# Softmax of the gate logits in PSUM: maxima, subtraction by an identity matmul and exponential per 510-column unit; residual kept in SBUF; clamp on GpSimd

## The reference, cut to what matters

```
h = layernorm(x) * (1 + ca) + sa
n = rmsnorm(h, norm_w)                                  # M = 16, H = 8
v = n @ W_v.T                                           # 128 values
gates = softmax((n @ W_a.T).reshape(B, T, H, M, M + 1)) # 128 rows of 17 logits per token
new = A_t @ state + a0 * v                              # the scan: 512 steps over T, per batch and head
x = x + ga * (h + ys @ W_out.T)
h = layernorm(x) * (1 + cb) + sb
logits = h @ router_w.T + router_b; the best 4 of 8 experts, softmax of their logits
gate, up = split(h @ gate_up.T + bias); gate = min(gate, 7); up = clip(up, -7, 7)
act = (up + 1) * gate * sigmoid(1.702 * gate); y = sum of weight_e * (act @ down_e.T + bias_e)
x = x + gb * y
```

## Time and profile before

| | us |
|---|---|
| median of 3 runs | 946.82 (946.27 to 947.31) |
| the profiled execution, whole | 945.81 |
| its span | 944.1 |
| mean granted TensorE clock | 0.818 of full |
| busy DVE, TensorE, ScalarE, GpSimd | 836.2, 641.1, 529.3, 517.0 |

### The profile page before, as it was taken

The page is one execution under the profiler, slowest core; times in us unless marked ns, Lnnn a source line. Parts: engine busy times, 40 slices in busy tenths (PEclk is TensorE's granted clock), DMA queues, the critical chain, the costliest instruction groups (busy, mean ns, idle before and its releaser), DMA issues.

```text
span 944.1 us, 11922 instructions
## 1 busy us (share of the span) xinstructions
PE 641.1 (68%) x2762; PEld 477.6 (51%) x2762; DVE 836.2 (89%) x2441; ACT 529.3 (56%) x1203; POOL 517.0 (55%) x539
## 2 busy tenths in 40 slices
PE   5544243585869767675859777676859777677786
PEld 4211022363646556464646555464647556566686
DVE  3455999999999999999999999999999999998753
ACT  3443321475765746475666746475766756364686
POOL 0584655574756565674756565574756464531243
PEclk9875665697977978697977978797978977797998
DMA  7035755554636353555636353545537352552000
GB/s 210 23 82 118 159 104 116 109 112 96 134 70 144 67 111 73 113 111 101 128 70 148 66 114 73 109 108 107 122 70 148 62 133 53 112 112 48 19 15 7
DMA packets 101670, 91.60 MB, mean 97 GB/s; under 512 B 43688, under 2 KB 98272, under 8 KB 99424
## 3 DMA queue, kind: packets, MB, share of 16 engines
q1 hardware_dynamic: 101600, 90.84, 45.4%
HBM read 46.76 MB, written 41.94 MB: 94 GB/s over the span
## 4 chain that ended last, share of the span: by engine, by line
DVE 67%; PE 16%; issue 7%; POOL 4%; SPq 2%; DMA 2%; ACT 2%; DVEq 0%; POOLq 0%; ACTq 0%
DVE prod L758 16%; DVE ps L766 15%; DVE zs L741 8%; DVE act_t L844 7%; DVE up L831 6%; DVE nmax L734 6%; PE ps L997 6%; PE ps L1010 5%; PE ps L984 3%; PE ps L1043 2%; DVE rz L749 2%; DVE xh L728 2%; ACT up L598 1%; POOL rs L393 1%; DMA gu_rows<-_L_ffn_gate_up_proj_dram 1%
## 5 line engine op out<-in xcount | busy, mean ns | idle before, releaser
L997 PE MATMUL ps<-h2t,wgu 128*128 128x256 f32 x1024 | 280.7, 424 | 0.6 <-ACT up L598 0.6
L1010 PE MATMUL ps<-wd,act_t 128*128 128x128 f32 x1024 | 168.6, 316 | 165.6 <-DVE act_t L844 165.6
L1010 PEld LDWEIGHTS ps<-wd,act_t 128*128 128x128 f32 x1024 | 150.5, 221 | 202.3 <-DVE act_t L844 190.0
L997 PEld LDWEIGHTS ps<-h2t,wgu 128*128 128x128 f32 x1024 | 218.4, 219 | 61.4 <-issue 29.8
L766 DVE TENSOR_REDUCE ps<-prod 64x16 f32<-64x272 f32 x512 | 220.1, 430 | 9.9
L758 DVE TENSOR_TENSOR prod<-gates,ps 64x272 f32<-64x272 f32 x512 | 213.9, 418 | 16.4 <-DMA gates<-gate_dram 14.3
L984 PE MATMUL ps<-wl,ht 128*128 128x512 f32 (+1 forms) x320 | 173.9, 649 | 53.1 <-ACT lg L581 43.1
L460 POOL TENSOR_TENSOR yacc<-yacc,weighted 128x256 f32<-128x256 f32 x128 | 94.2, 736 | 144.7 <-ACT weighted L615 144.7
L407 POOL TENSOR_TENSOR ex<-ex,rz 128x1088 f32<-128x1088 f32 x64 | 131.6, 2078 | 14.3 <-DVE rz L749 14.1
L414 POOL TENSOR_TENSOR lg<-lg,nmax 128x1088 f32<-128x1088 f32 x64 | 132.3, 2070 | 3.5 <-DVE nmax L734 3.5
L615 ACT ACTIVATE weighted<-ps,comb 128x128 f32<-128x128 f32 x256 | 79.8, 363 | 82.1 <-PE ps L1010 81.3
(11 more groups left out here) (119 smaller groups left out, 568.3 us busy)
## 6 DMA issues: line engine op xcount, KB each, us to landing
gate_dram<-ex SPq DMA_DIRECT2D x256, 136.0 KB, 3.0
gates<-gate_dram SPq DMA_DIRECT2D x32, 1088.0 KB, 8.3
yt_tok<-y_dram SPq DMA_DIRECT2D x256, 8.0 KB, 5.6
xg<-in_L_attn_x_dram SPq DMA_DIRECT2D x32, 64.0 KB
out_dram<-res SPq DMA_DIRECT2D x32, 64.0 KB
y_dram<-ys SPq DMA_DIRECT2D x32, 64.0 KB, 2.2
r_in<-out_dram SPq DMA_DIRECT2D x32, 64.0 KB
xm<-xn SPq DMA_DIRECT2D x16, 128.0 KB, 3.1
```

The source lines that it names most:

```text
L997: last = nc.tensor.matmul(gu_ps(m, k, which)[:, q * N:(q + 1) * N], wgu[:, k, rows + q * P:rows + (q + 1) * P], h2t[:, m % 2, :], start=Tr ...
L1010: last = nc.tensor.matmul(dn_ps(j), act_t[:, k % 2, q * N + j * P:q * N + (j + 1) * P], wd[:, k, q, :], start=(q == 0), stop=(q == KI - 1))
```

## The change

- Stages `g` and `e` become one: a tile's 128 rows of 17 logits are cut into five units (`unit`): four of 30 rows (510 columns) and one of 8 rows (136 columns, with the 128 columns of v beside it). A unit stays in one of three banks (0, 1, 7) until its exponential is read out.
- Per unit: TensorE makes the logits; DVE takes the negated maxima straight from PSUM (`row_max`); TensorE writes the negated maxima over the unit with an identity matmul whose moving operand repeats each maximum 17 times, and adds the logits by a second, equal matmul (`subtract`); ScalarE takes the exponential from PSUM with the rms factor as scale (`softmax_exp`). The copy to `lg`, the buffer and the subtraction on GpSimd are gone. The logits of unit n+3 stand behind `subtract` of unit n, in the same bank.
- There are six stages, 16 + 5 iterations, 13 of them full (4 to 16).
- The first half of an iteration is now the softmax on TensorE and ScalarE; experts 1 to 7, the output projection and the router come after it. Expert 0's `gate_up` stands behind unit 7.
- DVE takes row sums per unit, and `hidden` is one instruction of 512 columns. `clamp_up` is on GpSimd.
- `xg` has six buffers, `ht` four, `xn` three. The h part of the residual is added by an identity matmul of `ht` in the output projection's bank, x comes from `xg`; the residual's way over DRAM, `r_in`, `xm` and `res` are gone.
- SyncE stores and loads tile 0's gates before it turns to tile 1's.

The core of the diff:

```diff
+        def unit(n):
+            j, k = n // KL, n % KL
+            rows = min(RU, HI - k * RU)
+            return j, k * RU, rows, ps[:, (0, 1, 7)[n % 3], :]
...
-        DEPTH = 7
+        DEPTH = 6
...
+            def clamp_up(m, k):
+                pool.wait_ge(up_ok.sem, up_ok.at(m, k + 1))
+                nc.gpsimd.tensor_scalar(up[:, k % 2, :], up[:, k % 2, :], 1.0 + LIMIT, 1.0 - LIMIT,
...
+            def softmax_exp(g, n):
+                j, r0, rows, bank = unit(n)
...
+                act.wait_ge(sub_ps.sem, sub_ps.at(g, n + 1))
+                last = nc.scalar.activation(ex[:, j, r0 * M1:(r0 + rows) * M1], bank[:, 0:rows * M1], ACT.Exp,
+                                            scale=rms[:, j, :])
...
+            def between(u, a, g, p, m):
+                if g is not None:
+                    if u % 3 == 1 and u // 3 < NU:
+                        row_max(g, u // 3)
+                    if u in (20, 21, 23, 24, 26):
+                        row_sum(g, (20, 21, 23, 24, 26).index(u))
...
+                    if u in (33, 34, 36, 37, 38):
+                        row_sum(g, KL + (33, 34, 36, 37, 38).index(u))
...
+                    if u >= 42 and (u - 42) % 7 == 0:
+                        hidden(m, (u - 42) // 7)
...
+                    if u in (39, 41):
+                        j = (u - 39) // 2
...
             def logits(g, n):
...
+                if n >= 3:
+                    pe.wait_ge(exp_ok.sem, exp_ok.at(g, n - 2))
...
+            def subtract(g, n):
+                j, r0, rows, bank = unit(n)
+                pe.wait_ge(nmax_ok.sem, nmax_ok.at(g, n + 1))
+                w = rows * M1
+                nc.tensor.matmul(bank[:, 0:w].rearrange("p (r k) -> p r k", k=M1), ident[:, :],
+                                 nmax[:, j, r0:r0 + rows].unsqueeze(2).broadcast_to([P, rows, M1]), start=True,
+                                 stop=False)
+                nc.tensor.matmul(bank[:, 0:w], ht[:, g % RH, j * P:(j + 1) * P], wl[:, r0 * M1:r0 * M1 + w],
+                                 start=False, stop=True).then_inc(sub_ps.sem, 1)
...
+            def run(a, g, s, p, m, o):
+                if g is not None:
+                    for n in range(3):
...
+                        logits(g, n)
+                for n in range(NU):
+                    if g is not None:
+                        subtract(g, n)
+                        if n + 3 < NU:
+                            logits(g, n + 3)
```

More of the change, by code:

```diff
@@ L231, in adaln_block @@
         yt_ps, yt_ok, o_ps = event("yt_ps", 1), event("yt_ok", 1), event("o_ps", 1)
-        r_ld = [event(f"r_ld{j}", 16) for j in range(TILES)]
         go_ok, xn_ok = event("go_ok", TILES), event("xn_ok", 1)
@@ new lines, in store_gates @@
+            def store_gates(g, j):
+                sp.wait_ge(norm_ok.sem, norm_ok.at(g, 2 * j + 2))
+                sp.sem_inc(passed_sp, 1)
+                if not is_first(g):
+                    sp.wait_ge(g_ld[j].sem, g_ld[j].at(g, 0))
+                    sp.sem_inc(passed_sp, 1)
+                for b in range(B):
+                    sp.dma_start(gate_dram[j, b].rearrange("r t e -> t r e"),
+                                 ex[b * TS:(b + 1) * TS, j, :].rearrange("p (r e) -> p r e", e=ROW)
+                                 ).then_inc(g_st[j].sem, 16)
@@ new lines, in load_y @@
+            def load_y(s, j):
+                sp.wait_ge(y_st[j].sem, y_st[j].at(s, 16))
+                sp.sem_inc(passed_sp, 1)
+                if not is_first(s):
+                    sp.wait_ge(yt_ps.sem, yt_ps.at(s - 1, 1))
+                    sp.sem_inc(passed_sp, 1)
+                for b in range(B):
+                    sp.dma_start(yt_tok[b * TS:(b + 1) * TS, j, :].rearrange("t (h i) -> t h i", h=H),
+                                 y_dram[j, b].rearrange("h t i -> t h i")).then_inc(y_ld[j].sem, 16)
@@ L641, in run @@
                                                  ACT.Copy).then_inc(bias_ok.sem, 1)
-                        if k >= 1:
-                            weigh_expert(m, k - 1)
-                    if g is not None and k < KL:
-                        logits_out(g, 2 * k + 1)
-                    if k == 3 and a is not None:
+                for k in range(E):
+                    if m is not None:
+                        up_and_silu(m, k)
+                    if k == 0 and p is not None:
+                        act.wait_ge(yt_ps.sem, yt_ps.at(p, 1))
+                        nc.scalar.activation(yt[:, :], ps[:, 6, 0:N], ACT.Copy).then_inc(yt_ok.sem, 1)
+                    if m is not None and k >= 1:
+                        weigh_expert(m, k - 1)
+                    if k == 1 and a is not None:
                         act.wait_ge(h_ok.sem, h_ok.at(a, 1))
@@ L913, in run @@
                         scan_products(s, t)
-                    between(3 * t, a, g, e, p, m)
+                    between(3 * t, a, g, p, m)
                     if s is not None:
```

458 lines of the change are left out of this document (193 added, 265 removed).

## The result

| | before | changed |
|---|---|---|
| median, us | 947.07 (4 runs) | 1158.45 (1154.54 to 1162.49, 4 runs) |
| ratio | 1 | 1.2234, 95% interval 1.219 to 1.2278 |
| span of the profiled execution | 944.1 | 1155.7 |
| mean granted TensorE clock | 0.818 | 0.918 |
| a full iteration | 52.95, 12 of them | 67.09, 13 of them |

What follows compares the result with a forecast made beforehand. DVE's in-order stream bounded the old kernel, TensorE following. First scan step 77, iterations 2 and 3 48 and 51, 13 full ones of 63 (819), last scan's 40, tail 57.7, outside 1.7: 1095 us, range 1015 to 1165.

Steps and rivals of the forecast that it cites:

- the round trip: TensorE idle between a unit's subtraction and the logits reusing its bank, awaiting the exponential: 0.93 us, seven times a chunk.
- the residual in SBUF: Residual's way over DRAM dropped, three GpSimd vector instructions and six DMAs fewer: priced at nothing.
- waits at maxima: DVE waiting for logits up to the maxima of unit 9: 8 us, one wait per unit.
- start of `go`: DVE waits 4 us more for the output projection, until 36.9 us after scan step 0 starts (T); low clock adds 0.9.
- Behind hidden 0: DVE's own work from expert 0's `hidden` to the next iteration: 21.7 us, with 1.0 added for the low clock.
- The first logits at the low clock: Three logits opening an iteration on TensorE: taken at the high clock, 2.58 us, done at T+2.7.
- The forecast of DVE's busy time: DVE busy about 740 us over the span, against 836.2 before.
- The clamp: Clamp on GpSimd taken as 1.0 us and hidden; its removal saves DVE 4.3 us an iteration.
- 1 (overlap after all): Full iteration: waits overlap and DVE stays the bound at its own 47 us; 886 us total; chance 0.07.
- 2 (TensorE paces, DVE makes up its waits): Full iteration: TensorE sets the pace at 53 us, up to 57; 964 us total; chance 0.10.
- 4: Clamp on GpSimd costs 2.08 us and holds up `hidden`: iterations 66 to 69 us, 1150 total; chance 0.05 beyond the range.
- 3, the low clock in the softmax: TensorE's softmax half at the low clock: iteration 74 us, 1237 total; chance 0.06 for over 68 us.

Runs made afterwards that it cites:

- the projection alone: Changed kernel with `yt` evicted ahead of expert 0's up and Silu, and the output projection ahead of expert 1's gate_up: 1091.48 us, ratio 1.1541.
- the gate product alone: Changed kernel with GpSimd's last gate product moved behind the second layernorm's products: 1144.58 us, ratio 1.2084.
- the order is repaired: Changed kernel with logits of unit n+2 behind unit n, projection ahead of expert 0's Silu, last gate product behind the second layernorm: 986.64 us, ratio 1.0412.

## Why the prediction was right, and where its sum was off

**The sign and the mechanism.** 0.92 was put on slower, for the reason that the experiments bear out: the softmax as one row on TensorE holds up DVE at its maxima and `go`. The time, 1158, lies near the upper end of the range. Put in a row the runs divide the 211 us: 90 for the round trip (1158.5 to 1068.5), 77 for the place of `yt` and the projection (to 991.8), 5 for the gate product (to 986.6), 62 for the second matmul (to 924.7), and -22 for all else that the change brings. Another order of the steps gives other shares (the projection alone gave 67, the gate product alone 14), since they overlap. For "all else" only the clamp's place was measured by itself in the changed kernel; the residual in SBUF, priced at nothing, was not.

**Inside the iteration**, each step as it was put, and as measured from T:

| | predicted | measured |
|---|---|---|
| unit 7's subtraction | T+25.7 | T+26.6 |
| softmax off TensorE | T+31.3 | T+32.3 |
| waits at maxima | 8 | 8.2 |
| start of `go` | T+36.9, and 0.9 for the low clock | T+37.7 |
| hidden 0 done | T+39.5, and 0.9 | T+40.2 |
| next iteration | T+63 | T+66.0; 67.7 in eight of the 13 |

- *The round trip*: from the start of a unit's second logits to the logits behind the gap it is 1.88 us (452.79 to 454.67), with 0.86 and 0.93 predicted for the two, and the first matmul behind a gap takes 1.12, not 1.02. That is 0.2 a unit: 24.2 us from unit 0's subtraction to unit 7's, where I had 23.0. The block of three logits ahead was 0.3 shorter.
- *`go`* is right by two errors, in this iteration. The softmax was 1.0 late, and the low clock that I put on the projection (0.9) wasn't there yet: its four matmuls stand 0.22 to 0.32 us apart, from 486.06 to 486.83, the price at the high clock. It came behind them, as forecast, for the first down. In nine of the 13 iterations it was there at the first logits too, and `go` stood at T+38.8 to T+39.4.
- *Behind hidden 0* is **the step that failed**: "what is left of DVE's own: 21.7", with 1.0 for the clock, makes 22.7 from hidden 0 on, and it took 25.8 in this iteration. 1.5 of the 3.1 us is the second normalisation of `xn` (1.85 for 0.33), 0.4 the first (0.74), 0.4 its wait for the inverse root and 0.35 one for the router; the rest I can't place. The 1.0 for the clock was right: `hidden` 2 waited 0.91 for Silu. The rows of before couldn't show the collision (332 ns mean), but they gave its sign: the clamp's mean of 620 over its bare 409. I had read that as the price of a clamp, and a third of it was the price of meetings.
- *The first logits at the low clock* are **a second step that failed**: the sum had them at the high clock, to T+2.7. In eight of the 13 iterations the three logits took 4.0 to 4.4 us, for instance 4.19 (515.63) in place of 2.73 (449.37), at a PEclk of 0.77 in the stretch from 513 to 517, and these iterations are 1.7 us longer than this one; the first full iteration begins at the low clock as well. Ahead of them TensorE had waited 2.2 us for the last `hidden`, a wait that wasn't in the sum. But it had waited just as long ahead of the quick ones:

```profile
448.37 1.16 PE L985 MATMUL ps<-wd,act_t 128*128 128x128 f32 x8 [2.19 <-DVE act_t L813]
...
514.41 1.43 PE L985 MATMUL ps<-wd,act_t 128*128 128x128 f32 x8 [2.19 <-DVE act_t L813]
```

  So why the clock fell in one case and not in the other stays open.
- Of the 63 us the full iterations make 13 x 4.1 = 53: 1.0 of the 4.1 lies ahead of `go` in the mean (the low clock at the first logits), 3.1 behind it. The first scan step was at 76.86 (77 predicted), iterations 2 and 3 took 50.6 and 54.0 (48 and 51), the last scan's 37.7 (40), and what follows it 64.3 (57.7). Of DVE's waits for Silu 24.7 us lie there; what makes it 6.6 us longer I haven't followed up.

**The forecast of DVE's busy time** (about 740) missed: 796.1. 25 of the 56 us are the stretched normalisation (10.5 to 36.1 over the span). Most of the rest, I take it, is that records that overlap in a dense row count once in the busy time, and don't overlap where DVE waits. All DVE durations added up (count times mean) fell from 987 to 894 us, by 92; the busy time, in which an overlap counts once, fell by 40.

**The clamp** takes 0.61 us on GpSimd:

```profile
L448 POOL TENSOR_SCALAR up<-up 128x512 f32<-128x512 f32 x128 | 78.4, 612 | 170.0 <-ACT up L579 166.6
```

I took 1.0, nearer to a two-input row; the estimate that the prediction drew from the Trainium skill (GPSIMD Engine Reference, 3.1) was 0.6, and it holds. It changed nothing, since GpSimd had time, but "4.3 us less on DVE" was wrong on both sides: some 0.3 us a clamp where nothing meets it, and nothing of it in the time of a kernel that then waits elsewhere.

**Rivals.** 1 (overlap after all) and 2 (TensorE paces, DVE makes up its waits) fall with the 14.2 us of waits in an iteration; once the order is repaired, 2 is nearly what happens: 54.7 us an iteration against its 53 to 57. 4 falls with 0.61 us and the run that put the clamp back. 3, the low clock in the softmax, came in part: at its first logits, in nine of the 13 iterations (a PEclk of 0.50 to 0.54 over the first 3 us). From 6 us behind an iteration's start to its last unit the PEclk was 1.00 in all 13, for instance

```profile
461.00:465.00 4.00, 2.83 (x6) 1.06 (x6) 1.46 (x3) 1.08 (x2) 0.00 (x0) 1.00 0.11 29
```

with gaps of 0.78 us in it. The rule of the Trainium skill (TensorE: Matmul & The Clock Gate, on PSUM-queue cycling), by which short idle times between groups that cycle through banks make the clock go to and fro, didn't show at these gaps; where the clock fell in a full iteration, TensorE had idled for 2.2 us or more.

## What to carry to other kernels

Before work is moved between engines, write down for the new order on each queue what stands behind each wait: an idle time of 0.8 us for a round trip, repeated seven times in a row that everything else follows, cost 90 us here, and one unit of distance between a bank's release and its reuse took it away again. Work taken off the busiest engine is worth only what the next wait leaves: 47 us off DVE gave nothing by itself, and with one `hidden` for two and another order of GpSimd's queue the three gave 29. A short step on a chain (`yt`) belongs ahead of long ones on its engine, and counts nearly double where the idle time that it causes goes with a lower clock. And look at what a moved instruction leaves late: the gate product freed 17 us of DVE and made `hidden` wait 15.

## What the runs showed of the hardware

- A DVE normalisation of 128 elements, SBUF to SBUF, is held until a GpSimd instruction beside it is done: 1.85 us in place of 0.33, ending at 501.20 with GpSimd's product (501.13), which keeps its own 2.04. All 28 long ones of the changed kernel (0.40 to 1.86 us) end 0.08 us behind such a one; the 35 that had none beside them took 0.32 to 0.35. It goes the other way too: in the kernel before, 25 of GpSimd's 128 products and subtractions of this size began while a clamp was running on DVE, by 0.14 us and more, and these 25 alone took 2.21 to 2.22 us in place of 2.04. DVE's maxima, scan products and `hidden`, with an operand in PSUM, ran at their usual duration beside such products (for instance `hidden` at 495.98 took 0.69, beside a product from 495.33 to 497.37). The Trainium skill (SBUF — State Buffer, "SBUF: two separate sides") says that both engines share a pair of ports, held for a whole instruction by whichever of the two began first, while the other, if its kind of instruction needs them, is blocked. The trace agrees on the blocking. On who began first it agrees for those 25 and for the long one (GpSimd's record at 499.09, DVE's at 499.35), while at 498.35 DVE's record began 0.05 us ahead of GpSimd's and was still the one held.
- TensorE's clock stayed up through some 25 us of matmuls with gaps of 0.8 us in all 13 full iterations. It fell to 0.50 after the stretch from 485 to 489 in which TensorE was busy for 1.16 of 4 us, and in eight of the 13 also at the iteration's first logits, behind an idle time of 2.2 us that in the four short ones left it up. The first place cost 1.0 us an iteration through `hidden` 2, the second 1.7 where it came.
